# A DLRM tower on one core: the third layer with h2 as the standing operand, and y stored in two transfers

## The reference, cut to what matters

```
B, F, D = 2048, 26, 128
e  = stack([tbl_f[ids[:, f]] for f in range(26)], axis=1)      # B x 26 x 128
sd = einsum('bfd,bd->bf', e, dense)                            # 26 columns
ss = einsum('bfd,bgd->bfg', e, e)                              # pairs of fields
z  = concatenate([dense, sd, ss[:, iu, ju]], axis=1)           # 325 pairs
h  = concatenate([z, dense], axis=1)
h1 = maximum(h @ W_top1 + b_top1, 0)                           # B x 512
h2 = maximum(h1 @ W_top2 + b_top2, 0)                          # B x 256
y  = h2 @ W_top3                                               # B x 1
```

## Time and profile before

| | us |
|---|---|
| median of three executions | 377.8 |
| the profiled execution, device time | 375.83 |
| its span | 374.0 |
| PE matmul busy | 337.8 (90%) |
| PE weight loads busy | 312.3 (84%) |
| DVE busy | 243.8 (65%) |
| GpSimd busy | 246.3 (66%) |
| ACT busy | 187.7 (50%) |
| Y's matmul passes, 32 | 8.2 |
| y's copies on ACT, 8 | 3.3 |

### The profile page before, as it was taken

How to read it: one execution, slowest core, us unless ns; L and a number is a source line. 1 busy time by engine, 2 the same in 40 slices (tenths; PEclk the granted TensorE clock), 3 DMA queues, 4 the chain that set the end, 5 groups by cost and what they waited for, 6 DMA issues and landing times.

```text
span 374.0 us, 14392 instructions
## 1 busy us (share of the span) xinstructions
PE 337.8 (90%) x6278; PEld 312.3 (84%) x6278; DVE 243.8 (65%) x727; ACT 187.7 (50%) x270; POOL 246.3 (66%) x263
## 2 busy tenths in 40 slices
PE   0777867997999999999999999999999999989986
PEld 0765756997899989998999889989999898978874
DVE  1999959985596649754977478664984497511121
ACT  2343725563564456373754466545637365364532
POOL 5777676777777777777777777777777777720000
PEclk9999989998999999999999999999999999999999
DMA  7999652346533653364435443365335533340000
GB/s 172 251 240 244 202 153 73 105 108 143 128 115 93 142 142 99 89 144 125 113 82 129 127 130 105 95 147 136 107 92 133 131 107 89 74 110 16 4 2 0
DMA packets 41115, 43.92 MB, mean 117 GB/s; under 512 B 25614, under 2 KB 29946, under 8 KB 41052
## 3 DMA queue, kind: packets, MB, share of 16 engines
q1 hardware_dynamic: 32844, 26.20, 27.3%
q0 software_dynamic: 8192, 16.79, 17.6%
q10 hardware_dynamic: 16, 0.01, 0.0%
HBM read 38.12 MB, written 4.85 MB: 115 GB/s over the span
## 4 chain that ended last, share of the span: by engine, by line
PE 75%; DVE 12%; ACT 6%; DMA 3%; issue 2%; SPq 0%; ACTq 0%; DVEq 0%
PE et_ps L571 36%; PE g_ps L590 12%; PE m_ps L545 10%; DVE one_hot L476 7%; PE et_ps L563 7%; PE m_ps L631 7%; DVE table_lo L465 3%; ACT et L390 2%; ACT et L398 2%; PE m_ps L640 2%; DMA idb<-ids_one_hot 2%; DMA et<-tbl_in 2%; PE et_ps L600 1%; DVE w_lo L461 1%; DVE w_hi L459 1%
## 5 line engine op out<-in xcount | busy, mean ns | idle before, releaser
L358 POOL DMA_INDIRECT rows<-tbl_in,idx x256 | 245.4, 959 | 83.4 <-issue 71.3
L476 DVE TENSOR_SCALAR one_hot<-idb,first_row 125x256 fp32r<-125x256 int32 x640 | 200.0, 384 | 61.3 <-DMA idb<-ids_one_hot 35.5
L571 PE MATMUL et_ps<-one_hot,table_hi 125*128 125x256 f32 x640 | 170.7, 302 | 20.9 <-DVE one_hot L476 20.8
L571 PE MATMUL et_ps<-one_hot,table_lo 125*128 125x256 f32 x640 | 163.0, 288 | 0.0
L571 PEld LDWEIGHTS et_ps<-one_hot,table_hi 125*128 125x128 f32 x640 | 125.5, 196 | 26.6 <-issue 14.8
L571 PEld LDWEIGHTS et_ps<-one_hot,table_lo 125*128 125x128 f32 x640 | 126.0, 197 | 0.0
L398 ACT COPY et<-et_ps 128x512 f32<-128x512 f32 x64 | 80.3, 1259 | 23.3 <-PE et_ps L563 22.7
L390 ACT COPY et<-et_ps 128x256 f32<-128x256 f32 x80 | 48.6, 728 | 56.4 <-PE et_ps L571 56.3
L590 PEld LDWEIGHTS g_ps<-et 128*27 128x27 f32 x4096 | 46.6, 104 | 20.7 <-ACT et L398 6.1
L590 PE MATMUL g_ps<-et 128*27 128x26 f32 x4096 | 56.4, 192 | 8.2 <-ACT et L398 4.7
L411 ACT COPY gram<-g_ps 128x416 f32<-128x416 f32 x32 | 29.5, 921 | 49.8 <-PE g_ps L590 45.5
(11 more groups left out here) (58 smaller groups left out, 205.8 us busy)
## 6 DMA issues: line engine op xcount, KB each, us to landing
idb<-ids_one_hot SPq DMA_DIRECT2D x40, 256.0 KB
gram_rows<-gram SPq DMA_DIRECT2D x28, 169.0 KB
rows<-tbl_in,idx POOLq DMA_INDIRECT x256
et<-tbl_in SPq DMA_DIRECT2D x6, 448.0 KB
xt<-dense_t SPq DMA_DIRECT2D x8, 128.0 KB, 2.5
raw<-tbl_in SPq DMA_DIRECT2D x2, 448.0 KB
gram<-tbl_in SPq DMA_DIRECT2D x2, 448.0 KB
zt_raw<-gram_rows SPq DMA_DIRECT2D x14, 48.0 KB
```

The costliest lines, as they stand in the source:

```text
L358: nc.gpsimd.indirect_dma_start(out=rows[:, i % ROW_RING, n, :], out_offset=None, in_=tables[GATHERED[k]], in_offset=bass.IndirectOffsetOnA ...
L476: nc.vector.tensor_scalar(one_hot[0:KP, at % OH_RING, :], idb[0:KP, pair % ID_RING, n % 2, :], first_row[0:KP, 0:1], float(k), ALU.subtrac ...
L571: last = nc.tensor.matmul(ps[:, n % 2 * CH:(n % 2 + 1) * CH], part[0:KP, n, k, :], one_hot[0:KP, at % OH_RING, :], start=k == 0 and part i ...
```

## The change

The roles of the operands in the third layer are exchanged. A piece of h2, 128 features by 128 samples, is loaded as the standing operand, and w3's column moves. The result of 128 samples is then one column on 128 partitions. For the two halves of a chunk and the two halves of the features that makes four matmuls, two for each output column. ACT copies two columns to a tile `y` of its own, 128 x 16, which holds the results of all chunks. The store is issued twice: at chunk 6 for the chunks 0 to 6, and at chunk 7 for that chunk. ACT's wait before it writes h2 is now for the third layer of the chunk before, in place of the store.

```diff
-        y = h2[0:1, 0, :]
+        y = sb("y", [128, NCH * 2])
...
                 if kind == "M":
                     act.wait_ge(h2_sums, c + 1)
-                    wait(act, y_out, c * 16)
+                    wait(act, y_sums, c)
...
                 if kind == "Y":
                     act.wait_ge(y_sums, c + 1)
-                    nc.scalar.copy(y, m_ps[1][0:1, 0:CH]).then_inc(y_copied, 1)
-                    act.wait_ge(y_copied, c + 1)
-                    act.dma_start(out[:, c * CH:(c + 1) * CH], y).then_inc(y_out, 16)
-            act.wait_ge(y_out, NCH * 16)
+                    nc.scalar.copy(y[:, 2 * c:2 * c + 2], m_ps[1][:, 0:2]).then_inc(y_copied, 1)
+                    if c >= NCH - 2:
+                        act.wait_ge(y_copied, c + 1)
+                        of = slice(0, NCH - 1) if c == NCH - 2 else slice(c, NCH)
+                        act.dma_start(out.rearrange("o (c h p) -> (o p) c h", h=2, p=128)[:, of, :],
+                                      y[:, 2 * of.start:2 * of.stop].rearrange("p (c h) -> p c h", h=2), allow_slow_non_contiguous=True)\
+                            .then_inc(y_out, 16)
+            act.wait_ge(y_out, 32)
...
                 if kind == "Y":
                     pe.wait_ge(h2_done, c + 1)
-                    for k in range(H2 // 128):
-                        last = nc.tensor.matmul(m_ps[1][0:1, 0:CH], w3s[:, k:k + 1], h2[:, k, :],
-                                                start=k == 0, stop=k == H2 // 128 - 1)
+                    for half in range(2):
+                        for k in range(H2 // 128):
+                            last = nc.tensor.matmul(m_ps[1][:, half:half + 1], h2[:, k, half * 128:(half + 1) * 128],
+                                                    w3s[:, k:k + 1], start=half == k == 0, stop=half == k == 1)
                     last.then_inc(y_sums, 1)
```

## The result

| | before | after |
|---|---|---|
| median, four executions each, us | 377.64 | 386.5 |
| lowest and highest, us | 376.52, 379.02 | 385.92, 389.6 |
| profiled execution, us | 375.83 | 386.27 |
| its span, us | 374.0 | 384.5 |

The ratio is 1.025 with a 95% interval of [1.0185, 1.0314]. The change makes the kernel 2.5% slower. The forecast was 379.2 us, with a range from 376.4 to 382.0.

What follows compares the result with a forecast made beforehand. PE was taken to bound the kernel, with 39.7 of 40.4 us of a chunk period. Terms 0.5 + 0 + 0.10 + 0.8 = +1.4 us on the 377.8 median gave 379.2 us, range 376.4 to 382.0.

Steps and rivals of the forecast that it cites:

- The Y step on PE: Third-layer matmuls of each chunk: eight load-and-matmul pairs at 0.12 us, 0.96 us a step, 0.10 us dearer than before.
- (b): Rival on the Y step: fp32 loads at one cycle a column, 0.33 us cheaper a step, total about 376.1; chance 0.1.
- (d): Rival on the Y step: one-column matmuls drain before the next load, 1.3 us dearer a chunk, 388; chance 0.03.
- The eight steps: Y steps over all chunks: +0.5 us for chunks 0 to 4, 0 for chunk 5, +0.10 each for 6 and 7.
- ACT: ACT's y copy takes 0.155 us instead of 0.36 and six store issues go; nothing counted in full periods.
- the chunk 5 gap: PE's wait of 0.32 us until 341.88 for a chain through ACT's Gram copy; changes cancel, 0.
- The first store: Store of 1,792 4-byte pieces at chunk 6: issue on ACT of 1.9 to 2.4 us, hidden, costing nothing.
- rival (a): First store's issue goes only as fast as pieces drain, 4.9 us, 2.4 beyond the cover: 381.6; chance 0.2.
- the cover of 2.5 us: Time at chunk 6 in which the first store's issue on ACT stays hidden; each us beyond lands on the end.
- The tail: After the last Y step: +0.10 sums, -0.21 copy, +0.9 for a final store landing in 2.35 us; total +0.8.
- The rule on small transfers: Skill's rule on element-wise descriptors and transfers under 512 B, weighed for the final store: sum 0.7 us higher, about 379.9.

Runs made afterwards that it cites:

- p1: Changed kernel's matmuls and copy, but stores as before, one 1 KB piece per chunk (constant data); ratio to the kernel before 0.9977.
- p4: Kernel before, matmuls and copies untouched, with the two new stores of 1,792 and 256 4-byte pieces (constant data); ratio 1.0376.
- r4: r3 with the old third-layer step, copy and one-row 1 KB store for chunk 7 alone; 375.33 us against 376.44, ratio 0.9983.
- r3: Changed kernel with every second sample of h2 in a standing operand, so both stores have 8-byte pieces; everything computed; ratio to before 1.002.
- q3: Changed kernel with both stores' 4-byte pieces 512 bytes apart in a scratch tensor, output not written; ratio to before 0.996.
- p3: Changed kernel with the last store as one 1 KB piece (constant data), first store as it is; ratio to before 1.0178.
- q4: Kernel before with the Y step's 256 samples moved in four quarters into four partitions, stored as four 256-byte pieces; ratio 1.0039.
- q2: Changed kernel without the first store, the last store's 256 4-byte pieces 512 bytes apart in a scratch tensor; ratio to before 0.9983.

## Why the prediction was wrong, point by point

- **The Y step on PE** was right. 0.12 a pair and 0.96 us a step were taken.

```profile
L648 PEld LDWEIGHTS m_ps<-w3s,h x64: 186/192/192, 136.2 to 375.9; 128*128 128x128 f32 x64
L648 PE MATMUL m_ps<-w3s,h x64: 169/250/271, 136.3 to 375.9; 128*128 128x1 f32 x64
```

```profile
216.99 0.97 PEld L648 LDWEIGHTS m_ps<-w3s,h 128*128 128x128 f32 x8
...
217.98 0.80 PEld L596 LDWEIGHTS g_ps<-et 128*27 128x27 f32 x64
```

  Eight loads of about 190 ns start 0.111 apart ((0.97 - 0.19)/7); from the first load to Gram's go-on it is 0.99 us against 0.86. The matmuls' median is 250, not 170, as if each one-column matmul waited for its own load, which the 104 ns of the earlier trace rows had priced. Rivals (b) and (d) fall with this row.
- **The eight steps** were summed right, but their sum did not show. p1, which has just them, gave 0.9977 where 1.002 was forecast. Most of it went in one stage: from Y of chunk 4 to Y of chunk 5 the kernel before takes 41.1 us and p4, with the same PE program, 40.2; after and p1 take 38.5 and 38.6. In that stage both of the former have two "issue" waits on PE at the same two instructions, which the changed PE program lacks.

```profile
PE m_ps L631 <- issue: 0.9, 1, 0.9
PE et_ps L563 <- issue: 0.8, 1, 0.8
```

  These are of the kernel before, from 305 to 340 us. They are 1.7 of the 2.6 us. The prediction took no account of them, and no run shows that the exchange of the operands is what avoids them. Other stages differ by as much as 0.6 us between two profiled executions (40.99 in p1 for 40.39 before, from Y of chunk 1 to Y of chunk 2), so 0.10 us a step can't be read from them.
- **ACT** was right: the copy takes 0.16 us in the tail (0.155 taken), the chunk 5 gap is 0.36 where 0.32 was.
- **The first store** is one of the two steps that failed: "1.9 to 2.4 costs nothing" priced it as time of ACT. Its issue took 0.42 us, below the low end of 0.9, and its packets 2.4 us instead of rival (a)'s 4.9, so rival (a) as it was put fell and the cover of 2.5 us was never needed. The stretch from chunk 6's Y step to chunk 7's, which the sum had 0.10 us longer, became 6.62 longer: PE stood for 4.41 us and then ran at the slow clock (2.0 us from the first turned group to Y of chunk 7: 16.17 for 14.18). The likely way is PE's supply of instructions. The queue view for 351.0 to 351.5 us shows one packet of the instruction queue between 791 of the store:

```profile
q10 hardware_dynamic: 791, 0.00, 70.8%
q8 instruction: 1, 0.02, 18.9%
```

  At the same 27 passes before the end of that Gram step PE waits in every kernel with the new matmuls: 0.33 to 0.73 us without a first store of pieces, 0.56 to 1.01 with one of 8-byte pieces or of pieces 512 bytes apart (r4, r3, q3), 4.27 and 4.41 with pieces 4 bytes apart (p3, after). That close writes delay it is shown, though for kernels of one PE program only: q4, with another, waits 2.37 us with no such store. In all eleven kernels with the new matmuls one packet of 16 KB of the instruction queue ends before this wait does. In the nine others PE goes on 1.2 to 2.0 us after the packet's end, in the change and in p3 4.8 and 5.3 us after it (packet ends at 352.64 and 351.16, PE goes on at 357.43 and 356.44). So the transfer itself was not slow; what came late came after it, as it did behind the last store. That PE waits there for these instructions, which count as there only when the writes ahead of them are done, fits these times and was not tried by itself.
- **The tail** is the other step that failed, by as much: "I take 2.35, +0.9", with 4.2 us as the high end. It was 8.1, +6.64. 2.35 was right for pieces 512 bytes apart. The prediction counted pieces and took its prices from rows in which every piece has 256 bytes or more; nothing in it asked where the pieces lie relative to each other. The rule on small transfers, weighed there at +0.7 us for the size of the pieces, pointed the right way without naming the cause: size alone cost nothing against 2.35, and the 5.75 us above it came with the distance.

## What to carry to other kernels

Price a store by the distance of its pieces in DRAM: neighbouring 4-byte results from different partitions took 7.25 to 9.6 us from issue to the end of the kernel, the same pieces far apart 2.4, one row 1.5. At the end of a kernel that is paid in full, and in the middle it can still reach an engine that doesn't wait for the store. A standing operand of 128x128 fp32 costs 0.11 us a pass when one column moves. A pass of 256 moving columns over a one-column operand took 0.215 us, so 128 columns cost about the same, and exchanging the operands of a 256-column product gains nothing.

## What the runs showed of the hardware that was not expected

- Issuing 1,792 pieces takes ACT 0.42 us and 256 pieces 0.38, while four Gram writes of 676 pieces took 4.08 us: the length of an issue does not follow the number of pieces. For one piece of 1 KB it lies anywhere from 0.21 to 0.50 us in p1.
- The granted clock fell to 0.50 near the end of a pause of PE of 4.4 us and stayed there for over 6 us of work, and in r3 it was 0.62 over the stretch behind PE waits of 0.82 and 0.98 us, while q2, with waits of 0.73 and 0.98 us at the same two places, kept 1.00.
- Sixteen passes of 64 columns into four partitions 32 apart ran in 0.36 us instead of the 0.86 of four passes of 256: they do run side by side. But the short matmuls behind them lost 0.28 of the 0.50 us.
